# GpSimd makes a group's output factors behind its token root, and VectorE keeps the norms

## The reference

```python
x = mobius_add(residual, expmap0(attn_t))          # first half
residual = x
xn = layer_norm(logmap0(x))
xm = expmap0(xn * (1 + sc_mlp) + sh_mlp)
ff = plin(plin(xm, w_f1, b_f1), w_f2, b_f2)        # plin: expmap0(logmap0(x) @ w + b)
ff_t = g_mlp * logmap0(ff)
return mobius_add(residual, expmap0(ff_t))         # and the kernel's output adds x

def mobius_add(x, y):   # x2, y2, xy: sums over the 256 values of a token
    num = (1 + 2 * xy + y2) * x + (1 - x2) * y
    den = (1 + 2 * xy + x2 * y2).clip(EPS)
    return num / den
```

## Time and profile before

| | |
|---|---|
| median of 3 runs | 765.38 us (765.11 to 765.99) |
| the profiled execution | 765.7 us, span 763.9 us |
| TensorE, matmul busy | 644.4 us, 84% of the span |
| VectorE busy | 654.1 us, 86% |
| ScalarE busy | 524.7 us, 69% |
| GpSimd busy | 347.0 us, 45%, 683 instructions |
| mean DMA rate | 141 GB/s |

### The profile page before, as it was taken

How to read it: one execution, slowest core, us unless ns; L and a number is a source line. 1 busy time by engine, 2 the same in 40 slices (tenths; PEclk the granted TensorE clock), 3 DMA queues, 4 the chain that set the end, 5 groups by cost and what they waited for, 6 DMA issues and landing times. The chain is left out here.

```text
span 763.9 us, 27111 instructions
## 1 busy us (share of the span) xinstructions
PE 644.4 (84%) x8419; PEld 464.3 (61%) x8433; DVE 654.1 (86%) x2171; ACT 524.7 (69%) x1563; POOL 347.0 (45%) x683
## 2 busy tenths in 40 slices
PE   4956889999999999999999997605669999999996
PEld 2645667777777777777777775402326566656664
DVE  2786788999999999999999997485998999999975
ACT  1123567777777777777777775334879989999874
POOL 1003556666666666666666665111234244234321
PEclk9978899999999999999999998656999999999999
DMA  9942876666666666666666665222444455445523
GB/s 321 359 116 57 141 131 137 146 141 143 141 147 142 145 142 147 141 141 144 147 140 147 144 133 113 50 70 70 124 124 133 139 158 163 149 132 166 164 72 110
DMA packets 184804, 107.50 MB, mean 141 GB/s; under 512 B 140188, under 2 KB 167591, under 8 KB 184744
## 3 DMA queue, kind: packets, MB, share of 16 engines
q1 hardware_dynamic: 182952, 103.99, 55.6%
q10 hardware_dynamic: 1792, 2.89, 1.0%
HBM read 64.11 MB, written 9.18 MB: 96 GB/s over the span
## 5 line engine op out<-in xcount | busy, mean ns | idle before, releaser
L885 PE MATMUL p_qkv<-wqkv,tT 128*128 128x256 f32 x768 | 198.1, 396 | 5.5 <-DVE u L1143 5.5
L885 PEld LDWEIGHTS p_qkv<-wqkv,tT 128*128 128x128 f32 x768 | 139.7, 195 | 22.9 <-issue 6.3
L899 PEld LDWEIGHTS p_o<-v,pT 64*64 64x64 f32 x4096 | 66.7, 136 | 21.9 <-issue 21.9
L899 PE MATMUL p_o<-v,pT 64*64 64x17 f32 x4096 | 73.0, 210 | 0.0
L858 PE MATMUL p_oz<-wo,oT 128*128 128x256 f32 x256 | 69.7, 397 | 0.0
L445 POOL TENSOR_TENSOR rt<-ss_t,c_mhalf 128x1 f32<-128x1 f32 x64 | 42.1, 658 | 60.6 <-ACT junk L634 53.7
L659 ACT ACTIVATE pT<-p_s 128x1024 f32<-128x1024 f32 x64 | 65.6, 1024 | 2.8 <-PE p_s L875 1.7
L1143 DVE SCALAR_TENSOR_TENSOR u<-p_qkv,ct,bqkv 128x768 f32<-128x768 f32 x64 | 64.3, 1005 | 3.5 <-PE p_qkv L885 3.5
L617 ACT ACTIVATE oT<-p_oz 128x256 f32<-128x256 f32 x64 | 24.6, 384 | 57.0 <-PE p_oz L850 57.0
L504 POOL TENSOR_TENSOR rt<-ss,c_mhalf 128x2 f32<-128x2 f32 x32 | 26.5, 827 | 80.8 <-ACT wqkv L707 80.8
L933 PE MATMUL p_t<-ident,pT 128*128 128x128 f32 x128 | 21.3, 290 | 46.5 <-ACT pT L714 46.5
(11 more groups left out here) (275 smaller groups left out, 1685.2 us busy)
## 6 DMA issues: line engine op xcount, KB each, us to landing
mod<-mod_rows SPq DMA_DIRECT2D x128, 128.0 KB, 2.9
x_all<-in_x SPq DMA_DIRECT2D x8, 1024.0 KB, 14.3
gate<-mod_rows SPq DMA_DIRECT2D x128, 64.0 KB, 2.7
mod<-mod_rows SPq DMA_DIRECT2D x32, 256.0 KB, 4.2
mod_b<-mod_rows SPq DMA_DIRECT2D x32, 256.0 KB, 4.4
out<-x_all SPq DMA_DIRECT2D x32, 256.0 KB, 3.0
gate<-gate_rows SPq DMA_DIRECT2D x32, 128.0 KB, 2.9
bqkv<-gate_rows SPq DMA_DIRECT2D x32, 128.0 KB, 2.9
```

Source lines behind the costliest of these rows:

```text
L885: mm = pe.matmul(p_qkv[:, a * D:a * D + D], tT[:, k, c, :], wqkv[:, c, a * D:a * D + D], start=c == 0, stop=c == C - 1)
L899: mm = pe.matmul(p_o[S * e:S * e + S, col:col + VW], pT[keys, e, g, :], v[keys, k, 2 * g + e, :], start=True, stop=True, skip_group_check= ...
```

## The change

The 13 small operations of `output_factors` leave VectorE, where they stood at the end of the slot, and a chain of 14 on GpSimd takes their place at the end of GpSimd's slot, behind `token_roots2` of the same slot. Two operations with a fused multiply-multiply or add-add are written with the plain forms, the +1 is added earlier, and the reciprocal becomes a power of -1 with a new constant column `c_mone`. Each step of the chain signals `fac_step` and waits for it before the next, except `al2` and `be2`. `output_norms` and `output_root` stay on VectorE; `output_norms` now waits for `be2_ready` of the group before, as it overwrites the buffer that the chain reads.

```diff
@@ constants @@
+        c_mone = sb("c_mone", [P, 8])
+            pool.memset(c_mone[:, :], -1.0)
-        FIN_STEPS = 15
+        FIN_STEPS = 5
+        FAC_STEPS = 12
@@ gpsimd @@
+            def fac_op(g, k, ins):
+                ins.then_inc(fac_step, 1)
+                pool.wait_ge(fac_step, FAC_STEPS * g + (k + 1))
+            def output_factors(g, q):
+                pool.wait_ge(th_ready, g + 1)
+                after(pool, diag_ready, 4 * GROUP * (g - 1))
+                pool.wait_ge(xf_summed, 2 * GROUP * g + 2 * GROUP)
+                cf, f = fin[:, 0, :], lambda k: fin[:, k, :]
+                xx1, omx1 = (arrays[:, k, bass.ds(2 * GROUP * g, 2 * GROUP)] for k in (XX1, OMX1))
+                fac_op(g, 0, pool.tensor_tensor(f(5), th[:, :], ina[:, :], ALU.mult))
+                fac_op(g, 1, pool.tensor_tensor(f(6), f(5), cf, ALU.mult))
+                kap = f(6)
+                fac_op(g, 2, pool.tensor_tensor(f(7), kap, kap, ALU.mult))
+                fac_op(g, 3, pool.tensor_tensor(f(8), f(7), fst[:, q, 1, :], ALU.mult))
+                fac_op(g, 4, pool.tensor_tensor(f(9), kap, fst[:, q, 2, :], ALU.mult))
+                fac_op(g, 5, pool.tensor_scalar(f(9), f(9), 2.0, 1.0, ALU.mult, ALU.add))
+                fac_op(g, 6, pool.tensor_tensor(f(10), xx1, f(8), ALU.mult))
+                fac_op(g, 7, pool.tensor_tensor(f(11), f(9), f(10), ALU.add))
+                fac_op(g, 8, pool.tensor_scalar(f(12), f(11), EPS, None, ALU.max))
+                fac_op(g, 9, pool.tensor_tensor(f(13), f(12), c_mone[:, :], ALU.pow))
+                fac_op(g, 10, pool.tensor_tensor(f(14), f(9), f(8), ALU.add))
+                pool.tensor_tensor(al2[:, q, :], f(14), f(13), ALU.mult).then_inc(al2_ready, 1)
+                fac_op(g, 11, pool.tensor_tensor(f(5), omx1, kap, ALU.mult))
+                pool.tensor_tensor(be2[:, q, :], f(5), f(13), ALU.mult).then_inc(be2_ready, 1)
@@ gpsimd, end of slot2 @@
+                if group_at(h, off, M_P) is not None:
+                    output_factors(group_at(h, off, M_P), parity(off, M_P))
@@ vector, output_norms @@
                 after(dve, ina_ready, g)
+                after(dve, be2_ready, g)
@@ vector @@
-            def output_factors(g, q):
...
@@ vector, end of slot2 @@
-                if group_at(h, off, M_P) is not None:
-                    output_factors(group_at(h, off, M_P), parity(off, M_P))
```

More of the change, by code:

```diff
@@ L256, in build @@
         ff_squared = sem("ff_squared"); fg_squared = sem("fg_squared"); xf_summed = sem("xf_summed")
-        rf_ready = sem("rf_ready"); fin_step = sem("fin_step"); th_ready = sem("th_ready")
+        rf_ready = sem("rf_ready"); fin_step = sem("fin_step"); fac_step = sem("fac_step"); th_ready = sem("th_ready")
         ina_ready = sem("ina_ready"); al2_ready = sem("al2_ready"); be2_ready = sem("be2_ready"); diag_ready = sem("diag_ready")
```

## The result

The changed kernel takes 786.04 us (median of 4 runs, 782.26 to 786.69), the kernel before 765.25 us (4 runs, 763.61 to 765.99). The ratio is 1.0263 with a 95% interval of 1.0231 to 1.0295; in the series of experiments the same file gave 1.0301 (1.0260 to 1.0341). So the change costs 18 to 26 us. The prediction was 777.7 us, slower, with a range up to 785.5: the sign and about 12 of some 21 us are as forecast, and the median lies half a microsecond above the range.

A forecast was written before the change was run, and what follows sets the result against it. TensorE was taken as the floor, ScalarE nearly without slack. Five steady groups +8.7, first and seventh groups +0.5 each, end +2.6: together +12.3, so 765.7 + 12.3 - 0.3 = 777.7 us, range 770 to 785.5.

The forecast's parts named there:

- What bounds the kernel: Second part: TensorE runs without a gap in ordinary slots of 6.62 us; ScalarE has nearly no slack.
- What is removed: VectorE loses 13 operations, 2.49 us per group of four slots; TensorE's time gains only 1.28 us per group.
- The price of the chain: 14 operations on GpSimd: about 5.6 us in the steady part, 5.1 where VectorE is quiet; bounds 4.7 and 6.5.
- C: Length of GpSimd's chain of output factors, taken as about 5.6 us in the steady part.
- groups 1 to 5: The steady turns of four slots: a loss of 3.02 in place of 1.28 us, +1.74 each, +8.7 us.
- The loss per group: ScalarE's diagonals wait for `be2`, so its first square comes at +12.85 instead of +9.83 us, 3.0 us late.
- The formula: ScalarE's loss per group from waiting for `be2` is C - 2.58 us.
- group 0: First group (slot 7, not bound by TensorE): +0.5 us, bounds -1.5 and +2.
- group 6: Slots 31 and 32, the last tiles, with a chain of 5.1 us: +0.5 us.
- Rival 3: TensorE's granted clock falls after idle time ahead of the inner product, 5 x 1.5 = 7.5 us more: 785; 8%.
- The tail: Last group at the kernel's end, hidden by nothing: chain 5.08 in place of 2.49 us, +2.6 us.
- rivals 3 and 4: The fourth: small operations cost more than thought, C = 6.5, 785 us; 14%. The third has its own line.

The follow-up runs named there:

- e_best: Changed kernel with diagonals, sum and store one slot later, GpSimd's chain cut behind its ninth operation, and the last group's factors on VectorE: 755.61 us.
- e_fill: Changed kernel with ten extra bias matmuls on TensorE ahead of the real ones in each slot where ScalarE waits for `be2`: 777.81 us.
- e_split: Changed kernel with GpSimd's chain cut in two, the power and the rest coming behind `inner_roots` of the next slot: 795.63 us.
- e_swap: Changed kernel with ScalarE's copy of the transposed tiles ahead of the diagonals of tile 0: 788.63 us.
- e_lag: Changed kernel with the diagonals, the sum on TensorE and the store one slot later: 764.85 us, 1.0013 of the kernel before.
- c_after: Changed kernel run once more, unaltered, as yardstick of the experiments: 786.35 us.
- e_tail: Changed kernel with the last group's factors back on VectorE, the other groups staying on GpSimd: 779.36 us.
- e_nopow: Changed kernel with the power of -1 replaced by a product, so the output factors lack their division: 770.09 us.
- e_lagtail: Changed kernel with diagonals, sum and store one slot later and the last group's factors on VectorE, chain left whole: 764.72 us.

## Why the prediction was right or wrong

**What bounds the kernel.** Right. The steady slots of the changed kernel are 6.62 us again, and e_best, in which no wait reaches TensorE in these groups, comes to 6.65.

**What is removed.** Right: 1.25 us of TensorE's time per group and not 2.49. e_best gets 138.9 - 132.9 = 6.0 us back in five groups, 1.2 each.

**The price of the chain.** Right. C = 5.57 us measured (5.55 to 5.81 in groups 1 to 5), 5.6 predicted; 5.23 to 5.27 where VectorE is quiet, 5.1 predicted. Groups by line of the changed kernel (count, busy us, mean ns), which answer to the earlier trace rows:

```profile
L548 POOL TENSOR_TENSOR fin<-fin,c_mone 128x8 f32<-128x8 f32 x8 | 13.8, 1729 | 0.7
L547 POOL TENSOR_SCALAR fin<-fin 128x8 f32<-128x8 f32 x8 | 2.6, 322 | 0.7
L546 POOL TENSOR_TENSOR fin<-fin 128x8 f32<-128x8 f32 x8 | 2.4, 304 | 0.6
...
L549 POOL TENSOR_TENSOR fin<-fin 128x8 f32<-128x8 f32 x8 | 1.6, 200 | 0.6
```

A small operation takes 0.20 (0.19 taken), and 0.28 with its wait, two get 0.11 more beside VectorE's sums (0.31 and 0.35 against 0.20 and 0.24 where VectorE is quiet), a third 0.04, and the power of -1 costs as much as that of -0.5. The Trainium skill's ratio (GPSIMD Engine Reference, section 4.1 Engine selection: about twice as slow for two inputs) would have given 4.9 us, as an estimate; here the small operations alone were 0.28 against 0.20 us in spacing, and the power in place of VectorE's reciprocal, 1.73 against 0.20 us, made the chain 2.2 times as long.

**The loss per group.** Right at the upper clock. The formula with the measured seen time of `be2` (628.40 - 617.81 = +10.6) gives 10.6 + 2.15 - 9.83 = 2.9 us, and 29.43 - 26.48 = 2.95. e_fill, which holds the clock, needs 147.7 - 138.9 = 8.8 us more than before in groups 1 to 5 (predicted 8.7), 0.1 in group 0 (0.5) and 0.8 in group 6 (0.5). Group 0 is no clean comparison, since there the clock fell in the kernel before as well (0.75 in slot 8) and not in e_fill. That ScalarE's wait decides and not VectorE's `ch` is shown by e_split, that it is ScalarE's time and not one blocked inner product by e_swap, and that it is this wait by e_lag.

**The clock.** Here a step of the prediction failed: the sum put the clock at nothing. Rival 3 had the mechanism and gave it 8%, with the condition of a C of some 7 or of a fall at shorter idle times than the 2.69 us that had left the matmuls quick. The second condition held. The clock fell at 2.02 to 2.42 us, in three of five groups in each of three profiles (after, c_after, e_tail), and at 3.11 to 3.54 us in all five (e_split); at 1.03 to 1.19 us (e_nopow) and with the gap filled (e_fill) it fell in none. An inner product at the lower level takes 1.7 us longer (4.97 against 3.27), but the group loses about 1.0 us and not 1.5, since in a quick group the next slot is 7.17 us long and has TensorE idle again, for 0.49 us ahead of its transposes, and in a slow one it is 6.47 us long. In groups 0 and 6 the changed kernel lost 2.3 and 2.5 us where +0.5 each was taken; e_fill puts 1.5 to 2.2 and 1.7 of that down to the clock.

One row of the kernel before with 2.69 us was too little to set a threshold from, and it was luck that it was quick. The same instructions with the same idle time stand in slot 3 of all twelve profiles. In three (before, after, e_lagtail) the granted clock of that slot was 1.00, in nine it was 0.76 to 0.78, as here in c_after:

```profile
534.95 0.66 PE L966 MATMUL p_t<-ident,pT 128*128 128x128 f32 x4 [2.69 <-ACT pT L747]
...
536.29 4.97 PE L980 MATMUL p_qkv<-wff,qk 128*128 128x512 f32 x8 [0.26 <-ACT qk L752]
```

**The tail.** The second step that failed, by size: +5.1 us where +2.6 was forecast. The chain itself was right: VectorE's last sums start 769.03 - 755.06 = 13.97 us after the last `hh`, in place of 754.79 - 743.57 = 11.22. But I had followed only VectorE. The end of the changed kernel:

```profile
769.72 1.22 PE L992 MATMUL p_o<-x_all,ident 128*128 128x256 f32 x2 [4.28 <-ACT z L777]
...
773.29 1.06 PE L993 MATMUL p_o<-g_all,o 128*128 128x256 f32 x2
...
774.96 0.60 ACT L782 ACTIVATE x_all<-p_o 128x512 f32<-128x512 f32 x1 [4.23 <-PE p_o L994]
```

Pair 28 still goes through TensorE, which has been idle for 4.28 us (1.55 in the kernel before) and does its matmuls at 1.06 us for two in place of 0.59; so ScalarE's last evacuation ends at 775.56, after VectorE's sums, which end at 774.62, and the stores of the last four pairs leave in order behind it. In the kernel before that evacuation ended 1.38 us ahead of the sums. e_tail takes all 5.1 us back.

**The sum.** With the clock held (e_fill), 777.8 was measured for 777.7 forecast; but the two agree partly by chance, since the tail cost 2 us more than forecast there, and the kernel before took 1.4 us less beside it than the 765.38 that the forecast starts from. By stretches, the changed kernel's 21 to 22 us are 9.7 for the waits (9.7 forecast), 5.1 for the tail (2.6 forecast) and 6 to 7 for the clock, which was not in the sum. The upper end of the range stood for rivals 3 and 4, a fall of 1.5 us in each of five groups or C = 6.5. Neither size came true, so it is partly luck that the median lies so near to it.

## What to carry to other kernels

An engine with idle time is not a free place for work: ask first what stands behind the moved chain in that engine's order and what stands behind each consumer's wait, and move the consumer's lag and split the chain together with the work. Here the same move cost 2.6 to 3.0% as written and gained 1.1% with the lag and the queue put right and the last group's factors left on VectorE. And where TensorE is the bound, an idle time in front of it costs its own length and possibly a stretch at the lower clock as well; here 3 of the 11.7 us that five groups lost.

## What was not expected of the hardware

- Idle times of TensorE of 2.02 to 2.42 us, inside an otherwise full stretch, were followed by the lower level of the granted clock in nine of fifteen cases, in other groups in each of three profiles and not rather behind the longer ones; 1.03 to 1.19 us in none of five. Ten matmuls for nothing in the gap (e_fill) were worth 8.5 us of the median.
- The same work ahead of hh(2) took 525.4 to 532.1 us over twelve profiled executions, and the five slots behind it 30.0 to 33.4 us. The medians of the kernel before agree within 0.2% over four series, but one profile against another, as a whole, can't show a few microseconds.
- GpSimd's 8-column operations took 0.20 us alone and mostly 0.30 to 0.43 us beside VectorE's operations on two fp32 tiles of SBUF. The Trainium skill (Advanced Engine Details and Errata, VectorE Performance Modes) speaks of two-port modes; these rows show it with plain two-input operations too.
